# Attention with a feed-forward branch on one core: a q head's three rotation products become three entries of VectorE's planned order

## The reference, cut to what matters

```python
xn = layernorm(x)                                   # x: 2 x 1024 x 512, float32
q = (xn @ Wq.T) -> 32 heads of 128                  # k: 8 heads, part of it through a low rank
q = q * cos + rotate_half(q) * sin                  # the same for k
scores = q @ k.T / sqrt(128), causal
attn = softmax(scores)                              # 4 q heads share one k/v head
out = (attn @ v) @ Wo.T
x = x + out + (silu(xn @ Wgate.T) * (xn @ Wup.T)) @ Wdown.T
```

## Time and profile before

| | |
|---|---|
| median of 3 runs | 2445.08 us (2443.59 to 2448.58) |
| profiled execution: its time | 2448.94 us |
| profiled execution: its span | 2446.7 us |
| TensorE matmul busy | 2349.5 us, 96% of the span |
| VectorE, ScalarE, GpSimd busy | 1479.9, 1130.7, 938.3 us |
| instructions of TensorE, VectorE | 11840, 3641 |

### The profile page before, as it was taken

One profiled execution on the slowest core, in us unless ns is written; L12 is line 12 of the kernel. 1 busy time (PEld: TensorE's weight loads), 2 busy tenths in 40 slices (PEclk: granted clock), 3 DMA queues, 4 the chain that ended last, 5 costly groups with the idle time before them and its releaser, 6 DMA issues.

```text
span 2446.7 us, 38968 instructions
## 1 busy us (share of the span) xinstructions
PE 2349.5 (96%) x11840; PEld 1974.1 (81%) x11840; DVE 1479.9 (60%) x3641; ACT 1130.7 (46%) x2217; POOL 938.3 (38%) x813
## 2 busy tenths in 40 slices
PE   6999999999899999999999999999999999999998
PEld 5777877777788878888887888788878878888887
DVE  5343334424676667666676767676666766676765
ACT  2442624335454445444454545354445444454544
POOL 1000000000554454545454545455444545454543
PEclk9999999999999999999999999999999999999999
DMA  5676757689412122231313152312222131313110
GB/s 198 189 291 177 259 168 242 233 274 319 149 53 95 47 93 77 71 104 36 111 37 105 35 194 84 120 44 95 69 80 94 45 105 44 104 35 113 35 52 18
DMA packets 103880, 287.26 MB, mean 117 GB/s; under 512 B 9072, under 2 KB 42352, under 8 KB 92528
## 3 DMA queue, kind: packets, MB, share of 16 engines
q1 hardware_dynamic: 101552, 280.53, 34.2%
q10 hardware_dynamic: 2112, 4.19, 0.4%
HBM read 200.80 MB, written 83.89 MB: 116 GB/s over the span
## 4 chain that ended last, share of the span: by engine, by line
PE 69%; issue 4%; DVE 3%; ACT 2%; POOL 2%; DMA 1%; SPq 1%; DVEq 0%; ACTq 0%; POOLq 0%
PE ob L1161 16%; PE scores L1137 14%; PE qb L1119 14%; PE ob L1176 13%; PE ptb L1148 9%; DVE pT L1071 1%; PE ring L893 1%; PE ring L878 1%; DMA ff_raw<-in_ffw 1%; ACT pT L1024 1%; SPq L605 1%; PE down L902 0%; POOL late_qT L993 0%; POOL q_cos L989 0%; DVE q_sin L1066 0%
## 5 line engine op out<-in xcount | busy, mean ns | idle before, releaser
L1024 ACT ACTIVATE pT<-ptb 128x512 fp32r<-128x512 f32 x576 | 335.2, 594 | 526.5 <-PE ptb L1148 519.3
L1161 PE MATMUL ob<-pT,v_sb 128*128 128x512 f32 x1728 | 479.5, 406 | 15.1 <-DVE pT L1071 15.1
L1071 DVE TENSOR_TENSOR pT<-ptb,pT 128x512 fp32r<-128x512 f32 x576 | 390.6, 688 | 119.0 <-ACT pT L1024 108.8
L989 POOL TENSOR_TENSOR q_cos<-q_cos,q_sin 128x512 f32<-128x512 f32 x125 | 161.5, 1292 | 565.9 <-DVE q_cos L1067 565.9
L983 POOL TENSOR_TENSOR long_prob<-long_prob,rinv 128x384 f32<-128x384 f32 (+3 forms) x256 | 304.4, 1201 | 171.3 <-DVE rinv L1089 170.6
L1161 PEld LDWEIGHTS ob<-pT,v_sb 128*128 128x128 f32 x1728 | 304.8, 189 | 70.5 <-DVE pT L1071 23.8
L1119 PE MATMUL qb<-xT,wq 128*128 128x512 f32 x1488 | 359.9, 391 | 0.0
L983 POOL TENSOR_TENSOR short_prob<-short_prob,rinv 128x512 f32<-128x512 f32 (+3 forms) x256 | 278.4, 1095 | 197.7 <-DVE rinv L1089 195.2
L1137 PE MATMUL scores<-kT,late_qT 128*128 128x384 f32 (+3 forms) x1536 | 343.8, 359 | 1.4
L1119 PEld LDWEIGHTS qb<-xT,wq 128*128 128x128 f32 x1488 | 280.8, 189 | 60.1
L1137 PEld LDWEIGHTS scores<-kT,late_qT 128*128 128x128 f32 x1536 | 264.0, 188 | 29.0 <-issue 5.0
(11 more groups left out here) (95 smaller groups left out, 2978.0 us busy)
## 6 DMA issues: line engine op xcount, KB each, us to landing
wq<-w_parts SPq DMA_DIRECT2D x126, 512.0 KB, 3.9
w_parts<-stage SPq DMA_DIRECT2D x32, 1024.0 KB, 4.9
ff_raw<-in_ffw SPq DMA_DIRECT2D x56, 384.0 KB, 3.8
k_parts<-stage SPq DMA_DIRECT2D x128, 128.0 KB, 2.4
v_parts<-stage SPq DMA_DIRECT2D x64, 256.0 KB, 3.6
w_raw<-in_wqo SPq DMA_DIRECT2D x32, 512.0 KB, 5.8
kT<-k_parts SPq DMA_DIRECT2D x16, 1024.0 KB, 7.3
v_sb<-v_parts SPq DMA_DIRECT2D x16, 1024.0 KB, 9.0
```

The source lines that it names most:

```text
L989: nc.gpsimd.tensor_tensor(qc, qc, qs, ALU.add).then_inc(q_turned, 1)
L1024: nc.scalar.activation(pT[:, t % 4, HI], ptb[t % 2][:], ACT.Copy).then_inc(pT_hi, 1)
L1071: nc.vector.tensor_tensor(pT[:, t % 4, LO], ptb[t % 2][:], pT[:, t % 4, HI].bitcast(F32), ALU.subtract).then_inc(pT_split, 1)
L1161: mm = nc.tensor.matmul(ob[:], v_sb[e % 2][:, x, j], pT[:, t % 4, y], start=(j == 0 and (x, y) == (HI, HI)), stop=(is_last(kind, n, j) and ...
```

## The change

VectorE's entry `("dve", "Q")` of planned cost 1.97 becomes three entries, `QA` and `QB` of 0.65 and `Q` of 0.67, with urgency 3 as before. Each issues one of the three products. The waits stand in front of the first, and `q_read`, on which GpSimd's addition and the next Q product wait, is signalled by the third. TensorE's order is not touched. The instructions are the same and as many as before.

```diff
-URGENT = {"T": 0, "PV": 0, "W": 0, "NORM": 0, "INV": 1, "QL": 1, "EXP": 2, "S": 2, "Q": 3}
+URGENT = {"T": 0, "PV": 0, "W": 0, "NORM": 0, "INV": 1, "QL": 1, "EXP": 2, "S": 2, "Q": 3, "QA": 3, "QB": 3}
@@ followers
     if kind == "Q":
-        return [("dve", "Q", n, j, 1.97, 0.05), ("pool", "Q", n, j, 1.1, 0.1),
+        return [("dve", "QA", n, j, 0.65, 0.03), ("dve", "QB", n, j, 0.65, 0.03), ("dve", "Q", n, j, 0.67, 0.05), ("pool", "Q", n, j, 1.1, 0.1),
                 ("act", "QL", n, j, 0.55, 0.1), ("pool", "QL", n, j, 1.1, 0.1)]
@@ heads_vector
-                    elif kind == "Q":
+                    elif kind in ("QA", "QB", "Q"):
                         x = n // AHEAD % 2 * CHUNK
                         cos, sin = (qtab[:, i, x:x + CHUNK] for i in range(2))
-                        dve.wait_ge(q_done, it1 * UNITS + n + 1)
-                        if not opening or n >= AHEAD:
-                            dve.wait_ge(q_split, it1 * UNITS + (1 if opening and n == AHEAD else n))
-                        elif n == 1:
-                            dve.wait_ge(xT_stored, 16 * (CHUNKS + 1))
+                        if kind == "QA":
+                            dve.wait_ge(q_done, it1 * UNITS + n + 1)
+                            if not opening or n >= AHEAD:
+                                dve.wait_ge(q_split, it1 * UNITS + (1 if opening and n == AHEAD else n))
+                            elif n == 1:
+                                dve.wait_ge(xT_stored, 16 * (CHUNKS + 1))
                         bank = query_bank(n, opening)
                         qc, qs = turning(n, opening)
-                        nc.vector.tensor_tensor(qs[0:HALF], bank[HALF:P], sin[HALF:P], ALU.mult)
-                        nc.vector.tensor_tensor(qs[HALF:P], bank[0:HALF], sin[0:HALF], ALU.mult)
-                        nc.vector.tensor_tensor(qc, bank[:], cos, ALU.mult).then_inc(q_read, 1)
+                        if kind == "QA":
+                            nc.vector.tensor_tensor(qs[0:HALF], bank[HALF:P], sin[HALF:P], ALU.mult)
+                        elif kind == "QB":
+                            nc.vector.tensor_tensor(qs[HALF:P], bank[0:HALF], sin[0:HALF], ALU.mult)
+                        else:
+                            nc.vector.tensor_tensor(qc, bank[:], cos, ALU.mult).then_inc(q_read, 1)
```

## The result

| | before | after |
|---|---|---|
| median | 2445.9 us, 4 runs (2443.59 to 2448.58) | 2465.96 us, 4 runs (2462.72 to 2471.41) |
| ratio, 95% interval | | 1.0084 (1.0063 to 1.0105) |
| profiled execution, its span | 2448.94, 2446.7 | 2465.06, 2462.8 |

The account below looks back on a forecast made before the run. TensorE's fixed order, its matmuls busy for 96% of the span, was taken as the bound. 13.8 + 5.3 + 0.3 + 0 - 2.5 = 16.9 us on the 2445.1 median gave 2462.0, range 2449 to 2472.

Parts of the forecast that it names:

- the q chain: VectorE's products, GpSimd's addition, QL on ScalarE and GpSimd, into S(4,3): no slack, 0.86 us later per five-block step.
- the three orders worked: Planned sequences: QA, QB, S, QC on VectorE; addition, NORM, QL on GpSimd; one-block step QA, S, QB, T, INV, QC.
- TensorE's new row: Sign expected: scores waiting for GpSimd's late_qT in the five-block step, 10 to 14 us, 16 times.
- Five-block step: Maximum between products and NORM ahead of QL make S(4,3) 0.86 us later, 16 times: 13.8 us lost.
- One-block step: S, T and INV among the products delay ScalarE's QL and the second T copy by 0.33, 16 times: 5.3 us.
- Other steps: Two-, three-, four-, six-, seven- and eight-block steps: taken at nothing, the sum carrying 0.3 us; T(0,3)'s wait stays.
- Returns: Six returns of the loop: one late signal replaces another, 0 us, with bounds of -10 to +9.
- VectorE's return decides: Rival: cut right before the W addition exposes VectorE's return, 6 x 1.5 = 9 us more, 2471; chance 0.17.
- Opening: Once: S(0,3) goes behind QA and NORM(0,3) ahead of GpSimd's addition; -2.5 us, bounds nothing and -4.8.
- QL keeps its place: Rival: NORM does not get ahead on GpSimd, S(4,3) late by only 0.4, 16 times; 2449 us; chance 0.09.
- The waits for pT go: Rival: earlier T entries end the 20.5 us of PV and T waits; -9.2 us, 2436; chance 0.07.
- The order stays: Rival: no entry ready in the gaps of 0.11, so three entries act as one; 2445 us; chance 0.04.

Follow-up runs that it names:

- Experiments 1 to 3: Changed kernel with the q head one entry again ahead of the five-block step, the one-block step, or both: 2454.1, 2458.95 and 2447.53 us.
- experiment 4: Changed kernel with GpSimd's QL put ahead of NORM in the five-block step: 2460.33 us, ratio 1.0051.
- experiment 3: Changed kernel with the q heads ahead of both the five-block and one-block steps one entry again: 2447.53 us, ratio 0.9992.
- e1: Changed kernel with only the q head ahead of each five-block step one entry again: 2454.1 us, ratio 1.0011.
- e2: Changed kernel with only the q head ahead of each one-block step one entry again: 2458.95 us, ratio 1.0041.
- e3: Same run as experiment 3: changed kernel, q heads ahead of five-block and one-block steps one entry again; 2447.53 us, ratio 0.9992.
- e6: Changed kernel with one entry again at n % 16 >= 6, keeping the changed kernel's cuts at the loop's returns: 2448.66 us, one execution.
- e12: Same run as experiment 5: changed kernel, five-block step's third q product behind INV and the W addition; 2528.84 us, one execution.
- e5: Same run as experiment 4: changed kernel with GpSimd's QL ahead of NORM in the five-block step; 2460.33 us, ratio 1.0051.
- experiment 8: Same run as e9: changed kernel, one entry again at n % 8 = 5, 6, 7, plus three order moves; 2448.44 us, ratio 1.0005.
- e9: Changed kernel, one entry again at n % 8 = 5, 6, 7, plus three order moves in the five-, three- and one-block steps: 2448.44 us, ratio 1.0005.
- experiment 5: Changed kernel with the third q product moved behind INV and the W addition in the five-block step: 2528.84 us, one execution.

## Why the prediction came out right, point by point

**Direction, place and mechanism.** Right. The prediction held that the q chain ahead of the five-block step had no slack (S(4,3) began 0.13 behind it) and that S(k,0), being ready in the gap, would get between the products. Both are in the trace, as are the three orders worked. Experiments 1 to 3 take the loss away by undoing these two steps alone. TensorE's new row was expected at 10 to 14 us and is 16.3.

**Five-block step.** 0.86 a step predicted, 0.93 measured. The two parts that it names, the maximum and NORM, are 0.52 and 0.42 by experiment 4.

**One-block step.** The mechanism was right, the size too small: 0.33 a step predicted, 0.46 measured in PV(2,1). The mis-sized term is the start of the last product. It was put 2.18 behind the start of QA, with the entries packed as closely as before; the trace has it 2.42 behind. Of that 0.24, 0.18 reaches ScalarE's QL (4.50 after QA, 4.32 predicted) and the T copy behind it (5.03, 4.84 predicted).

**Other steps.** Right at nothing for the split itself: experiment 3, which keeps the split there, is at 0.9992. T(0,3)'s wait stayed (0.27 and 0.28 a step in the two traces), as said.

**Returns.** 0 predicted with -10 to +9; the profile has +1.5, the mean over seven kernels is some +3. The exchange of one late signal for another is in the rows. That its two sides, 8 to 10 us each, come out so nearly equal was assumed and not worked out: the mechanism was foreseen, the small sum was luck. The rival "VectorE's return decides" was right in its mechanism (PV(1,0) now waits for the W addition), not in its sum, because ScalarE's return got cheaper by about as much.

**Opening.** -2.5 predicted. S(1,1) and T(0,0) did come earlier, and in the profiled executions of e1, e2, e3 and e6, which have the same opening, it is worth -2.0 to -2.4 (in e12 -1.7). Those of after and of e5 kept only 0.3 and 0.2. After's timeline and one stretch say why:

```profile
626.89 3.32 PE L1141 MATMUL scores<-kT,early_qT 128*128 128x384 f32 x9 [3.49 <-DVE nmax L1050]
```
```profile
628.00:634.00 6.00, 5.36 (x22) 4.60 (x22) 4.09 (x18) 4.30 (x12) 5.24 (x6) 0.50 0.09 36
```

Behind the idle stretch TensorE ran at 0.50, the 1.2 GHz level, for these 6 us. The stretches that lie likewise behind the wait in before, e1 and e5 read

```profile
634.00:640.00 6.00, 4.51 (x24) 3.33 (x24) 3.53 (x17) 4.42 (x12) 5.38 (x6) 0.80 0.01 1
```
```profile
634.50:640.50 6.00, 4.94 (x26) 4.07 (x25) 4.26 (x19) 4.77 (x13) 5.56 (x7) 0.79 0.11 46
```
```profile
629.00:635.00 6.00, 5.36 (x22) 4.60 (x22) 4.17 (x18) 4.29 (x12) 5.15 (x6) 0.50 0.16 64
```

The wait is 3.49 in after, e1 and e5 alike (4.79 in before), so what it brings differs between executions: where the clock came back as early as in before, the gain stayed; where it stayed low, the gain was lost.

**The sum.** 16.9 predicted, 20.1 measured, 20.2 by step. Against the forecast the steps are off by +0.9, +0.6, +1.5, -1.9 and +2.2. Some of the closeness is chance: without the half-clock stretches in before's trace the one-block step would stand at 7.3 against 5.3, and the opening's missing gain differs from execution to execution. The two worked mechanisms together cost 22.3 where 19.1 had been forecast.

**The other rivals.** "QL keeps its place": it did not; experiment 4 forces it, and 8.3 of the 14.95 remain, 0.52 a step where the rival had 0.4. "The waits for pT go": they rose from 20.5 to 22.4. "The order stays": excluded by the timelines.

## What to carry to other kernels

An engine that frees itself earlier helps only if what it does next is awaited. Where the bounding engine has a fixed order, find for each signal how long before its use it arrives. A signal with 0.1 us to spare pays for what is put ahead of it, except where another wait of the chain gets shorter: here a maximum of 0.8 us cost 0.52 and, through another engine's queue, a NORM of 1.25 us cost 0.42; a split that looks like freedom for the planner ("other work may stand between") lengthens just that chain. The same list of slacks shows where to gain: give the chain without slack the first place on each engine, and look at what then stands behind a later wait in an in-order queue (INV in experiment 8, e9) before counting the gain.

## What the hardware showed that I had not expected

An idle stretch costs more than its length once the clock falls behind it: 3.14 us of waiting (experiment 5) brought a further 1.9 us a step ((9.0 of PV(3,0) + 8.0 of Q + 13.6 of S(5,0)) / 16), with the granted clock at 0.52 for 2.9 us and 0.90 for the next 3, while 1.03 us of waiting left it at 1.00. Between the two it went either way: in the attention of before, three of the waits of 1.8 to 2.4 us had the clock at 0.50 behind them for over 3 us, and others of 2.1 us did not. Each such stretch cost 0.8 to 1.6 us in the comparison of before and after, and it moves from one execution to the next. And each engine pays its return of the loop by itself, 1.6 to 2.2 us in the returns shown; which of them TensorE feels depends on what stands first behind each cut, and the sum over six returns stayed within -0.9 and +5.2 us of the kernel before however the cuts lay.
